# Spreading the key indices by 21 wider products between key matmuls, and another order at the beginning and in the first tile

## The reference, cut to what matters

```python
x = x + attention(x, Wq, Wk, Wv, Wo, k_blocks, v_blocks, block_tables, kv_lens)
x = x + einsum('bct,bcd->bdt', x, weights[subjects])    # layer 1: one 64x64 matrix per sequence
h = einsum('bsi,ji->bsj', x, Wt)                        # layer 2
z = einsum('bsj,brj->bsr', h, A[i2])                    # rank 16, i2 picked per sequence
x = x + einsum('bsi,oi->bso', x, W_base) + einsum('bso,po->bsp', einsum('bsr,bor->bso', z, B_w[i2]), Wp) * scaling[i2]
x = x + einsum('btd,od->bto', x, W) + einsum('btr,bor->bto', einsum('btd,brd->btr', x, A3[i3]), Bm[i3]) * scalings[i3]
```

## Time and profile before

| what | value |
|---|---|
| median of 3 runs | 530.87 us (526.93 to 531.74) |
| profiled execution | 531.22 us, its span 529.4 us, so 1.8 us lie around the span |
| PE busy in the span | 482.3 us (91%) |
| DVE, ACT, POOL busy | 307.3, 247.8, 235.6 us (58, 47, 45%) |
| mean granted TensorE clock | 0.967 |
| DMA | 64.79 MB, mean 122 GB/s |

### The profile page before, as it was taken

How to read it: one execution, slowest core, us unless ns; L and a number is a source line. 1 busy time by engine, 2 the same in 40 slices (tenths; PEclk the granted TensorE clock), 3 DMA queues, 4 the chain that set the end, 5 groups by cost and what they waited for, 6 DMA issues and landing times.

```text
span 529.4 us, 10822 instructions
## 1 busy us (share of the span) xinstructions
PE 482.3 (91%) x2959; PEld 337.8 (64%) x2959; DVE 307.3 (58%) x895; ACT 247.8 (47%) x633; POOL 235.6 (45%) x252
## 2 busy tenths in 40 slices
PE   3999999898988998998999998998989899989996
PEld 1346955545666676675777676766767666767674
DVE  2889316643665664746466655747375637566641
ACT  0332122314544554655556655545465636555551
POOL 1465115651535455555355455555444445535200
PEclk9999579999989999999999999999899979999999
DMA  7456339632455353545445443535344434464131
GB/s 207 127 184 204 105 119 269 217 84 63 127 159 136 76 144 75 139 93 137 131 112 136 105 125 84 137 86 136 87 132 111 107 103 118 118 147 120 30 64 41
DMA packets 73226, 64.79 MB, mean 122 GB/s; under 512 B 49685, under 2 KB 49941, under 8 KB 73202
## 3 DMA queue, kind: packets, MB, share of 16 engines
q1 hardware_dynamic: 58160, 35.87, 25.8%
q0 software_dynamic: 14400, 28.05, 19.9%
q10 hardware_dynamic: 642, 0.60, 0.4%
HBM read 70.27 MB, written 10.22 MB: 152 GB/s over the span
## 4 chain that ended last, share of the span: by engine, by line
PE 64%; issue 10%; DMA 9%; DVE 6%; POOL 4%; ACT 3%; SPq 2%; another core or an unknown queue 1%; POOLq 1%; DVEq 0%; ACTq 0%
PE gb L1051 13%; PE sbk L1201 7%; PE ob L1225 6%; PE tb L1214 6%; PE gb L1056 6%; PE gb L1044 5%; DMA windows<-kvrows_dram,idx_b 4%; PE ob L1044 4%; PE tb L1121 3%; PE tb L1187 3%; PE gb L1246 3%; PE gb L1263 2%; DMA kvc<-kvl_dram 1%; POOL windows L509 1%; PE ob L1139 1%
## 5 line engine op out<-in xcount | busy, mean ns | idle before, releaser
L509 POOL DMA_INDIRECT windows<-newkv,idx_b x96 | 98.7, 1028 | 166.7 <-DMA windows<-kvrows_dram,idx_b 78.5
L932 DVE CUSTOM_DVE_ANT_0 wide<-sbk,mask 128x336 f32<-128x336 f32 x128 | 60.2, 504 | 83.3 <-issue 38.4
L668 ACT ACTIVATE wide<-wide,negmax 128x336 f32<-128x336 f32 x128 | 73.0, 573 | 33.0 <-DVE negmax L932 23.8
L674 ACT ACTIVATE pt_s<-tb 112x384 f32<-112x384 f32 x128 | 55.8, 487 | 45.2 <-PE tb L1214 35.2
L1201 PE MATMUL sbk<-kt_s,qt_s 64*128 64x336 f32 x256 | 56.7, 501 | 15.0 <-issue 13.8
L1044 PE MATMUL gb<-wkv_s,xt_s 128*128 128x512 f32 x120 | 56.1, 621 | 1.3 <-ACT kvo L598 1.3
L1214 PE MATMUL tb<-cst,wide 128*112 128x128 f32 x384 | 53.2, 274 | 0.3 <-ACT kt_s L662 0.3
L1225 PE MATMUL ob<-pt_s,windows 112*64 112x128 f32 x768 | 51.7, 286 | 0.0
L1225 PEld LDWEIGHTS ob<-pt_s,windows 112*64 112x64 f32 x768 | 43.7, 142 | 10.1 <-issue 7.2
L1214 PEld LDWEIGHTS tb<-cst,wide 128*112 128x112 f32 x384 | 43.1, 133 | 8.7 <-issue 3.1
L945 DVE TENSOR_SCALAR wide<-wide,rinv 128x336 f32<-128x336 f32 x128 | 45.5, 397 | 2.8 <-DVE rinv L939 0.5
(11 more groups left out here) (185 smaller groups left out, 879.4 us busy)
## 6 DMA issues: line engine op xcount, KB each, us to landing
xt_s<-xt_dram SPq DMA_DIRECT2D x31, 256.0 KB, 4.1
newkv<-kvo SPq DMA_DIRECT2D x16, 256.0 KB, 3.1
xtok_s<-xtok_dram SPq DMA_DIRECT2D x16, 256.0 KB
out_dram<-xo SPq DMA_DIRECT2D x16, 256.0 KB, 4.6
down_sel<-down_tab SPq DMA_DIRECT2D x64, 32.0 KB
up_sel<-up_tab SPq DMA_DIRECT2D x64, 32.0 KB
windows<-newkv,idx_b POOLq DMA_INDIRECT x96
wkv_s<-wkv_dram SPq DMA_DIRECT2D x4, 256.0 KB, 8.9
```

Source lines behind the costliest of these rows:

```text
L509: nc.gpsimd.indirect_dma_start(kv_s[r][:, c, :], None, newkv, bass.IndirectOffsetOnAxis(ap=idx_b[r][:, 2 + c:3 + c], axis=0), bounds_check ...
L668: nc.scalar.activation(prob[i][:, g, :], neg_s[:, g, :], ACT.Exp, bias=negmax[:, g:g + 1], scale=-1.0, accum_out=psum_p[i][:, g:g + 1]).th ...
L674: nc.scalar.activation(pt_s[g][:], tb[g % 2][0:KP, 0:CH * 128].rearrange("p (c q) -> p c q", c=CH), ACT.Copy).then_inc(S["pt_ev"], 1)
L932: V.tensor_tensor_reduce(out=neg_s[:, g, :], in0=sbk[g % 2][:, 0:WK], in1=mask[(t.part(u) + k) % 2][:], scale=-1.0 / 16, scalar=3.0e38, op ...
```

## The change

1. The 56 index matmuls of 32 columns become 21: 14 blocks with three columns of indices side by side (96 moving columns) and 7 with two (64). They stand in threes behind each of the four matmuls of `key_tile(8)` and `key_tile(9)`. What the constant matrices did before (half of even rows, even, odd) three POOL operations and one changed one do now on the rows themselves (`pair_rows`, `single_rows`, signal `rows1_ready`).
2. Constants are in three parts: a small early one (116 columns), a late one (600 columns) and the few-row one; the last two and two of the `xt_s` loads wait for the first weights.
3. ACT copies key tiles 0 and 1 before the sines and evacuates `blkrow` before it squares them.
4. `queries_t(1)` goes behind `key_tile(12)`; POOL adds both identities after root 14; `m23` uses banks `tb0, tb1, ob0, ob1` instead of `tb1, ob0, ob1, tb0`; the `down3` product is cut in two with scores between; `carried(3)` uses `ob[1]`, and `queries_t` of the first tile waits for one carried table instead of four.
5. SP stores `down3` and loads the picked parts of layer 1 and `down` at the start of the first tile, the `up` parts later; three semaphores instead of one tell PE which has landed.

```diff
-            key_tile(8)
-            pe.wait_ge(S["rows_ready"], 1)
-            pe.wait_ge(S["rows0_ready"], 1)
-            lay_index(0, 0, "pair_half", 0, PAIRS, 8)
...
-            last = lay_index(4, 1, "single", PAIRS, SINGLES, 16)
-            key_tile(9)
+            key_tile(8, 0)
+            key_tile(9, C)
...
+            def lay_index(part):
+                if part == 0:
+                    pe.wait_ge(S["rows0_ready"], 1)
+                    pe.wait_ge(S["rows1_ready"], 1)
+                for n in range(INDEX_PART * part, min(INDEX_PART * (part + 1), WS)):
+                    if n < PAIRS:
+                        begin = 8 * (PAIRS - 1 - n)
+                        last = mm(tb[0][0:KP, 0:CH * NB], con("pair", BLOCK)[:, begin:begin + KP],
+                                  pair_rows[:, n].rearrange("p k b -> p (k b)"), start=(n == 0), stop=(n == PAIRS - 1))
...
+                if n == 2:
+                    pool.wait_ge(S["rows_ready"], 1)
+                    fresh = fresh_rows.rearrange("p (s b) -> p s b", b=NB)
+                    for k, parity in ((1, "even"), (2, "odd")):
+                        P.tensor_scalar(pair_rows[:, :, k, :], fresh[:, 0:PAIRS, :], con(parity, BLOCK), None, ALU.mult)
+                    P.tensor_copy(single_rows[:, :, 1, :], fresh[:, PAIRS:WS, :]).then_inc(S["rows1_ready"], 1)
                 root("k", 4, n + 4)
...
-            for i in range(1, 4):
+            load_xt(1, 1)
+            sp.wait_ge(l_wkv[2], 16)
+            for i in range(2, 4):
                 load_xt(i, i)
...
             act.dma_start(cst[0][:], const).then_inc(S["l_const"], 16)
+            act.wait_ge(l_wkv[0], 16)
+            act.dma_start(cst[2][:], constl).then_inc(S["l_late"], 16)
             act.dma_start(cst[1][:], constf).then_inc(S["l_few"], 16)
...
-                if n == 14:
-                    add_identity(w3_s, ("l_w3", 16 * C + 32), "w3_ident")
+                    add_identity(w3_s, ("l_w3", 16 * C), "w3_ident")
...
-                dense((tb[1], ob[0], ob[1], tb[0])[k][:], lambda c: wb_s[:, c, 128 * k:128 * k + 128],
+                dense((tb[0], tb[1], ob[0], ob[1])[k][:], lambda c: wb_s[:, c, 128 * k:128 * k + 128],
...
-            pe.wait_ge(S["m23_lo"], C)
+            pe.wait_ge(S["m23_lo"], 2)
             keys_t(t0, 0, 0)
             pe.wait_ge(S["k_copied"], TILES - 1)
-            narrow(gb[0], 128, lambda c, k: wb_s[:, c, 128 * k:128 * k + 128], lambda c: a3_s[:, c, :]).then_inc(S["down3_mm"], 1)
-            scores(t0, 0, 0, range(G))
+            pe.wait_ge(S["l_ab3"], 32)
+            narrow(gb[0], 128, lambda c, k: wb_s[:, c, 128 * k:128 * k + 128], lambda c: a3_s[:, c, :], range(2))
+            scores(t0, 0, 0, (0, 1))
+            narrow(gb[0], 128, lambda c, k: wb_s[:, c, 128 * k:128 * k + 128], lambda c: a3_s[:, c, :],
+                   range(2, C)).then_inc(S["down3_mm"], 1)
+            scores(t0, 0, 0, (2, 3))
...
-                pe.wait_ge(l_pick[(t.c + 1) % 2], picked_at(t))
+                picked(t, "w1", 32)
```

More of the change, by code:

```diff
@@ L49, in constants @@
 def constants():
-    t = [np.zeros((rows, n), np.float32) for rows, n in zip((128, NB), NCONST)]
+    t = [np.zeros((rows, n), np.float32) for rows, n in zip((128, NB, 128), NCONST)]
     def put(name, a):
@@ L79, in constants @@
     x = np.arange(PAIR_W)[None, :]
-    for name, odd, value in (("pair_half", 0, 0.5), ("pair_even", 0, 1.0), ("pair_odd", 1, 1.0)):
-        put(name, value * ((off % 2 == odd) & (x == 8 * (PAIRS - 1) + off // 2)))
+    put("pair_times", BLOCK / 2 * (off % 2 == 0))
+    put("pair_plus", off / 2 * (off % 2 == 0))
+    put("even", off % 2 == 0)
+    put("odd", off % 2 == 1)
+    put("pair", x == 8 * (PAIRS - 1) + off // 2)
     put("single", np.arange(SINGLE_W)[None, :] == 16 * (SINGLES - 1) + off)
@@ L116, in build @@
 def build(nc, xt, xtok, kvrows, wkv, wq, wo, qs, ks, w1, wb, wt, a2t, b2t, wpt, s2, w3, a3t, b3t, s3,
-          table, kvl, picks, const, constf, out):
+          table, kvl, picks, const, constf, constl, out):
     f32, i32, f16, f32r = mybir.dt.float32, mybir.dt.int32, mybir.dt.float16, mybir.dt.float32r
@@ L290, in build @@
         kv_new = [sem(f"kv_new{i}") for i in range(4)]
-        l_pick = [sem(f"l_pick{i}") for i in range(2)]
+        l_pick = {w: [sem(f"l_pick_{w}{i}") for i in range(2)] for w in ("w1", "down", "up")}
         block = ctx.enter_context(nc.Block())
@@ L417, in tile @@
                 after(sp, S["out_mm"], t.n(1, -1))
-                load_picked(t)
+                load_picked(t, layer=not first)
             tile(Tile(0, 0), True, False, True)
@@ L888, in _ @@
                 link(V.tensor_scalar(none[:, HW * i:HW * i + HW], w, 0.0, float(NONE), ALU.is_equal, ALU.mult))
-                last = V.scalar_tensor_tensor(rows[:, 1, HW * i:HW * i + HW], w, -1.0, none[:, HW * i:HW * i + HW], ALU.add, ALU.add)
+                last = V.scalar_tensor_tensor(fresh_rows[:, HW * i:HW * i + HW], w, -1.0, none[:, HW * i:HW * i + HW], ALU.add, ALU.add)
             last.then_inc(S["rows_ready"], 1)
@@ L1062, in key_tile @@
                 after(pe, S["k_copied"], n - 1)
-                dense(gb[n % 2][:], lambda c: xt_s[r][:, c, :], lambda c: wkv_s[:, c, :]).then_inc(S["ka_mm"], 1)
+                for c in range(C):
+                    last = mm(gb[n % 2][:], xt_s[r][:, c, :], wkv_s[:, c, :], start=(c == 0), stop=(c == C - 1))
+                    if c == C - 1:
+                        last.then_inc(S["ka_mm"], 1)
+                    if index_from is not None:
+                        lay_index(index_from + c)
             def queries(count, bank):
@@ L1111, in _, with narrow @@
             key_tile(7)
-            key_tile(8)
-            pe.wait_ge(S["rows_ready"], 1)
-            pe.wait_ge(S["rows0_ready"], 1)
-            def lay_index(column, k, table, first, blocks, step):
-                width = con(table, BLOCK)
-                for s in range(blocks):
-                    begin = step * (blocks - 1 - s)
-                    last = mm(tb[0][0:KP, NB * column:NB * column + NB], width[:, begin:begin + KP],
-                              rows[:, k, NB * (first + s):NB * (first + s) + NB], start=(s == 0), stop=(s == blocks - 1))
-                return last
-            lay_index(0, 0, "pair_half", 0, PAIRS, 8)
-            lay_index(1, 0, "single", PAIRS, SINGLES, 16)
-            lay_index(2, 1, "pair_even", 0, PAIRS, 8)
-            lay_index(3, 1, "pair_odd", 0, PAIRS, 8)
-            last = lay_index(4, 1, "single", PAIRS, SINGLES, 16)
-            last.then_inc(S["idx_mm"], 1)
-            key_tile(9)
+            key_tile(8, 0)
+            key_tile(9, C)
             pe.wait_ge(S["split_lo"], C)
             queries(1, sbk[0])
-            def narrow(bank, width, lhs, rhs):
-                for k in range(C):
+            def narrow(bank, width, lhs, rhs, ks=range(C)):
+                for k in ks:
                     for c in range(C):
@@ L1147, in _ @@
             key_tile(12)
+            queries_t(1, sbk[1])
             key_tile(13)
@@ L1251, in ranks @@
                 pe.wait_ge(S["x2_ready"], t.n(1, 0))
+                picked(t, "down", 64)
                 dense(ob[1][0:64, 0:128], lambda c: down_sel[(t.c + 1) % 2][:, c], lambda c: x2t[:, c, :]).then_inc(S["z_mm"], 1)
```

152 lines of the change are left out of this document (89 added, 63 removed).

## The result

The changed kernel takes 511.63 us in the median of 4 runs (508.72 to 514.22), where before took 530.01 (526.93 to 531.74): the ratio is 0.9658, 95% interval 0.9579 to 0.9736. That is 18.4 us, or 3.4%, faster. The profiled execution of after took 514.22 us, its span 512.4 at a mean granted clock of 0.963; before's was 531.22, with a span of 529.4 at 0.967. Ratios in this document leave out executions more than 1.5% above the quickest of the same kernel; medians and averages count all.

What follows compares the result with a forecast made beforehand. PE, hardly ever idle to 134 us and at half clock around the index block, was taken as the bound. Terms -3.3, -16.0 (includes start), -4.8 to -20.8, then -0.9: -21.7 us, profiled 509.5, median 509; range 503 to 517.

Steps and rivals of the forecast that it cites:

- Start, -3.3: Up to 44 us: `blkrow` 1.8 us earlier and `kvc` 1.5 us earlier, together -3.3 us.
- `kvc`: Start: this load lands earlier with less queued before the weights; worth 0 to 3.9 us, taken as 1.5.
- The table load: Start: ACT's second load, 1.28 us, hidden while ACT awaits angles; without that cover it takes back 1.3 of 1.8.
- Index, -16: Index products: 42 records take 4.8 us instead of 18.21, key tiles at full clock; queries begin earlier, sum -16.0 us.
- The 2.3 us of waiting for DVE ahead of the queries: Before `queries(1)`: PE idles 2.3 us for DVE's fourth split, ready at 56.2 us, having left key tile 9 at 53.9.
- To the first tile, -4.8: Between queries and first keys: removed or filled waits give -0.7, -1.6, -1.4 and -1.1 us, bringing the sum to -20.8.
- All four waits: Before the first tile: waits for `qrot` 0.66, second identity 1.56, `m23` low part 1.41, third score 0.84 us go.
- DMA becomes late: Rival: without the block of 56, `stage` loads land later and key tiles wait 4 to 5 us; 514 us, chance 0.09.
- First two tiles, -0.9: Waits for carried tables, 1.29 us, and picked parts, 2.61, go; POOL's gathers late next, so 0.9 of 3.9 taken.
- Steady tiles, unchanged: Tiles after the first two: no change in their time.
- Low clock again: Rival: clock falls to 1.2 GHz around the index matmuls, costing about 7 us; 516 us, chance 0.13.
- Slower: Rival: low clock from key tile 8 held up to the first keys, 35 us slower, 566 us; chance 0.03.

Runs made afterwards that it cites:

- after_again: The changed kernel, unchanged, run and traced a second time; 504.5 us, ratio 0.954 to before.
- front_alone: Kernel before with the rearranged beginning alone: three constant tables, later loads, ACT's first two copies ahead of the sines; 525.5 us, ratio 0.993.
- one_block: Changed kernel with the 21 wide index products in one block behind key tile 8 instead of in threes between key matmuls; 507.2 us, ratio 0.965.
- before_again: The kernel before, unchanged, run and traced a second time; 527.5 us.
- The picks alone: Kernel before with only the picked parts' three semaphores instead of one, PE waiting for each ahead of its product; 528.5 us, ratio 0.986.

## Why the prediction was right, and where it was wrong

**The sum.** -21.7 us forecast, -18.4 measured. By its own rows, the part of -21.7 that was only clock is 18.21 less 112 x 0.094 = 7.7 in the block, 2.9 in key tile 9, 0.3 in the queries: 10.9. The other 10.8 is work and waits. Measured are 8.5 and 9.8. So the two totals were near; their places were not, and that the number came out is in part luck: the 10.9 were to come from the index block, and in the execution profiled the clock was as low there as before. At full clock the first keys come at 111 us in both traces of before and at 105 and 104 in those of after, 6 to 7 us earlier where the forecast had 20.8 - 10.9 = 9.9; the tiles, which were to give 0.9, made up for it with about 5.

**Start, -3.3.** `kvc` was right: 1.75 for 1.5. The Trainium skill (DMA: Bandwidth & Descriptors, section Queues, rings and completion order) lets a DMA engine go round its queues packet by packet; taken as in the prediction, that would have left `kvc` where it was. The trace has 1.75 us, and it decides. The table load took back 1.1 of `blkrow`'s gain (angles at 16.77, sines at 17.91): its cover was gone, which the prediction had priced at 1.3 and not taken. Wrong was the step that DVE "waits for it and then works without a pause, too: -1.8": in after it is busy with its own tables until 22.77, and `rows` comes 1.2 us earlier. In after_again `blkrow` is taken at 20.70 and `rows` is ready at 44.35, as before. In front_alone, at the first keys about 2 us arrive, at the end 0.7.

**Index, -16.** This is where the prediction failed most. The term "42 x 0.115 = 4.8 us in place of 18.21" set a block at the low clock against products at the full one, and so credited the index with a clock that it doesn't own. At equal clock it is 10.5 against 5.3 (42 x 0.125), and 2.7 to 4.9 are measured at the end. The price per record was right, 125 ns for 115. `rows1_ready` came 4.1 us late: 2.2 because `rows` was late (43.16 for 41.0), the rest mostly by the price of POOL's two operations, 1.70 us each where 0.73 was scaled from a row of 16x672. An operation of the same shape took 0.94 at 30.23 us, so the shape alone isn't the reason; what is wasn't tested. The Trainium skill (SBUF — State Buffer, section Who interferes with whom) has a rule that comes to mind: an operation of DVE with two inputs from SBUF and one of GpSimd that reads SBUF don't run side by side, the later one waits. The trace shows that it can't be all: DVE's last product ended at 45.47 us and DVE then stood idle until 48.01, yet POOL's second operation, from 45.03 to 46.65, took 1.63 us, and the pair took 3.39 or 3.40 in all eight traces that have it. Nor does the trace agree with it at 30.32 us, where DVE's product with two inputs took its usual 0.43 beside POOL's operation of 30.23 to 31.17. PE waited 2.96 us for them instead of 1. The 2.3 us of waiting for DVE ahead of the queries didn't come, since PE was late itself (one_block has 0.27 there).

**To the first tile, -4.8.** All four waits are gone, as said. A new one of 1.15 us (1.29 in after_again) for `b_s` came: the rival "DMA becomes late", in small.

**First two tiles, -0.9.** The two waits of 1.29 and 2.61 are gone but for 0.39 of the first, and PE waits 2.10 us for the gather instead (147.39 in after), as the step had it: from first to fourth keys 32.2 and 31.8 us in the two traces of before, 30.6 and 31.6 in those of after. The picks alone gave 3.7 at full clock, more than this step allowed them.

**Steady tiles, unchanged.** Nearly right, against what the two profiles seemed to show: from first to last keys at full clock 361 us in before_again and 356 in after_again, and 2.8 of the 5 between them are the wait for `up_sel` in the second tile.

**Low clock again** was given 0.13 at 516. In after's own trace it happened, with the first keys 6 us later than in after_again; the run took 514.2, and after_again's profiled execution, whose beginning has two low stretches of 7 us (from 40 and 84 us), 511.8. Both have a mean clock of 0.963. A low stretch in the beginning costs less at the end than at its place, because others come later either way: after_again lost 0.03 of its tiles' clock, after 0.02.

**Slower** wasn't seen: the longest low stretch in the beginning was 24 us, and in after it ended within the first queries.

## What to carry to other kernels

Price removed work at the clock that it would have had anyway, and keep the time lost to the clock as an account of its own: here 12 to 28 us are lost on average in every version, wherever they fall. Before explaining a difference between two profiles, look at a second profile of each; 8 us of 17 were an accident of one. Span times granted clock stays within 1% of its mean (498 to 506 for before) when times scatter by 2%. Two rounds of after differ in it by 1.9 us, so with four runs each it tells parts of about 4 us apart, not of 2. And follow a gain to the place where it is used: 2.5 us won at `blkrow` were 1.2 at `rows` and 0.7 at the end.
